# Turning the attention probabilities: TensorE transposes or one crossbar DMA a step

## The reference

```python
qk = jnp.einsum('bsd,btd->bst', q, k)                 # q = xn (8,512,256); 1024 keys
softmax_qk = jax.nn.softmax(qk * scale[:, None, :], axis=-1)   # scale: four rows of q, 1024 numbers a batch
attn = jnp.einsum('bst,btv->bsv', softmax_qk, v)
shared = new_gelu(xf @ Wfc_s + bfc_s) @ Wproj_s + bproj_s      # 256 -> 1024 -> 256
routed = sum over 8 experts e of gate_e * (new_gelu(xf @ Wfc[e] + bfc[e]) @ Wproj[e] + bproj[e])  # top 2 gates
out = x + attn + shared + routed
```

## Time and profile before

| | |
|---|---|
| median of three runs | 770.87 us |
| profiled execution, first to last instruction (span) | 769.0 us |
| the profiled execution's own time beside the span | the run's time is 770.87 us by the median: 1.9 us lie outside the span |
| TensorE busy / weight loads | 98% / 84% of the span |
| VectorE, ScalarE, GpSimd busy | 61%, 58%, 30% |
| DMA, mean over the span | 171 GB/s |

### The profile page before, as it was taken

The page is one execution under the profiler, slowest core; times in us unless marked ns, Lnnn a source line. Parts: engine busy times, 40 slices in busy tenths (PEclk is TensorE's granted clock), DMA queues, the critical chain, the costliest instruction groups (busy, mean ns, idle before and its releaser), DMA issues.

```text
span 769.0 us, 21389 instructions
## 1 busy us (share of the span) xinstructions
PE 756.3 (98%) x6963; PEld 645.5 (84%) x6963; DVE 470.6 (61%) x1161; ACT 449.6 (58%) x863; POOL 231.6 (30%) x272
## 2 busy tenths in 40 slices
PE   7999999999999999999999999999999999999998
PEld 6899866777777778999899988888888888888887
DVE  5887858888887797454544544444344444336776
ACT  6666546666668775556556565455544455544452
POOL 2445426656566752012122121121211221220000
PEclk9999999999999999999999999999999999999999
DMA  9657222657575958655523558546465646304565
GB/s 307 213 184 168 86 83 85 228 185 254 186 235 179 354 202 291 171 165 135 160 69 69 172 147 226 172 132 204 123 192 152 177 138 198 97 29 151 159 205 152
DMA packets 109949, 131.29 MB, mean 171 GB/s; under 512 B 64496, under 2 KB 91472, under 8 KB 103488
## 3 DMA queue, kind: packets, MB, share of 16 engines
q1 hardware_dynamic: 84784, 108.30, 46.4%
q0 software_dynamic: 6480, 17.77, 6.3%
q10 hardware_dynamic: 18624, 4.46, 2.9%
HBM read 89.32 MB, written 41.18 MB: 170 GB/s over the span
## 4 chain that ended last, share of the span: by engine, by line
PE 92%; DVE 3%; issue 2%; ACT 1%; DMA 1%; POOL 1%; ACTq 0%; DVEq 0%; POOLq 0%
PE ps_v L1413 32%; PE ps_h L1393 31%; PE ps_v L1573 11%; PE ps_h L1509 11%; PE ps_t L1523 4%; DMA slots_x<-x_split,pos_i 1%; PE ps_t L1344 1%; DVE h_split L1021 1%; PE ps_v L1471 0%; ACT h L804 0%; PE ps_v L1420 0%; PE ps_v L1344 0%; POOL slots_x L712 0%; PE ps_h L1445 0%; DVE v_split L1077 0%
## 5 line engine op out<-in xcount | busy, mean ns | idle before, releaser
L1021 DVE TENSOR_TENSOR h_split<-h,h_split 128x512 f16<-128x512 f32 (+1 forms) x224 | 142.3, 642 | 157.8 <-ACT h_split L810 157.6
L804 ACT ACTIVATE h<-ps_h,b_fc 128x256 f32<-128x256 f32 (+1 forms) x320 | 126.0, 444 | 156.2 <-PE ps_h L1393 156.2
L1393 PE MATMUL ps_h<-x_t,w_split 128*128 128x256 f16 (+1 forms) x1920 | 193.3, 261 | 0.1
L1413 PE MATMUL ps_v<-w_stage,h_split 128*128 128x256 f16 x1704 | 192.6, 273 | 0.2 <-DVE h_split L1021 0.2
L1393 PEld LDWEIGHTS ps_h<-x_t,w_split 128*128 128x128 f16 x1920 | 170.4, 98 | 17.4 <-issue 0.4
L1413 PEld LDWEIGHTS ps_v<-w_stage,h_split 128*128 128x128 f16 x1704 | 166.3, 98 | 19.5 <-issue 0.4
L748 POOL DMA_INDIRECT tokens_y<-prob,to_i x71 | 73.5, 1035 | 325.5 <-DMA tokens_y<-prob,to_i 177.6
L810 ACT CAST h_split<-h 128x512 f16<-128x512 f32 (+1 forms) x224 | 130.7, 584 | 10.0
L1509 PE MATMUL ps_h<-k_t,x_t 128*128 128x512 f16 x384 | 88.1, 379 | 1.7 <-issue 1.7
L1573 PE MATMUL ps_v<-v_split,p_t 128*128 128x256 f16 x768 | 88.9, 272 | 0.0
L804 ACT ACTIVATE h<-ps_h,b_t 128x256 f32<-128x256 f32 x128 | 53.5, 468 | 57.2 <-PE ps_h L1393 55.3
(11 more groups left out here) (162 smaller groups left out, 613.6 us busy)
## 6 DMA issues: line engine op xcount, KB each, us to landing
w_split<-wpack SPq DMA_DIRECT2D x17, 1024.0 KB, 5.7
w_stage<-wpack SPq DMA_DIRECT2D x17, 1024.0 KB, 5.3
wpack<-w_split SPq DMA_DIRECT2D x8, 1024.0 KB, 5.0
wpack<-h_split SPq DMA_DIRECT2D x8, 1024.0 KB, 5.0
y_rows<-tokens_y SPq DMA_DIRECT2D x32, 256.0 KB, 3.4
b_pj<-bias_e SPq DMA_DIRECT2D x40, 128.5 KB, 3.7
w_stage<-in_L_ffn_Wfc_dram SPq DMA_DIRECT2D x4, 1024.0 KB, 7.1
scale_b<-key_scale SPq DMA_DIRECT2D x8, 512.0 KB, 6.2
```

The lines of the kernel that those rows point to most:

```text
L804: ins = nc.scalar.activation(h32[:, hc, 0:n], ps_h[:, hc * TILE:hc * TILE + n], ACT.Gelu_apprx_tanh, bias=bias[:, hc:hc + 1], scale=1.0 / WS)
L1021: ve.tensor_tensor(h_split[par][:, 1, 2 * b:2 * b + 2, 0:n], h32[:, 2 * b:2 * b + 2, 0:n], h_split[par][:, 0, 2 * b:2 * b + 2, 0:n], ALU.s ...
L1393: ins = mm(ps_h[:, hc * TILE:hc * TILE + cols], wv[:, wl, c, hc * P:(hc + 1) * P], x[:, xl * DC + c, 0:cols], start=n == 0, stop=n == 3 * ...
L1413: ins = mm(ps_y[a][:, :], h_split[par][:, xl, c, a * P:(a + 1) * P], wv[:, wl, c, :], start=n == 0, stop=n == 3 * HC - 1)
```

## The change

The eight TensorE transposes of a step go away. ScalarE now casts `prob` straight into an SBUF tile `p_split` (hi), VectorE writes lo beside it (one instruction of 1024 columns in place of two of 512), and SyncE issues one DMA that turns both halves through the DMA crossbar, 128 rows of 4 KB, 512 KB, into `p_turned`, from which `values(u)` reads. `p_split` has two buffers, in the place of `w_shared[0]`; `p_turned` has three, the two old `p_t` and a part of `w_shared[1]`. The shared weights are therefore stored to DRAM (`w_rest`, 2 x 1024 KB) in the first stage and read back in the routed stage. The reciprocal of the row sum gets four buffers. The side work uses the PSUM tile `ps_t` again, which is free now, so its extra waits on `finish` go. The order within a step changes too: VectorE does `scale_scores(u+2)` first and `p_lo(u+2)` last in pass `u`, and ScalarE does `p_hi(u+2)` right after `exp(u+2)`, where before both halves of step `u` were made in pass `u`.

```diff
@@ dram
+    w_rest = dram("w_rest", (2 * P, 4096), f16)
@@ tiles
-        inv_sum = sb2("inv_sum", [P, 1], f32)
+        inv_sum = [sb(f"inv_sum{n}", [P, 1], f32) for n in range(4)]
+        p_split = [w_shared[0][:, n * 2 * KEYS:(n + 1) * 2 * KEYS] for n in range(2)]
+        p_turned = [t[:, :, :, :] for t in p_t] + [w_shared[1][:, 0:2 * KEYS].rearrange("p (h c n) -> p h c n", h=2, c=KC)]
-        side = [ps_v[:, a * 512:(a + 1) * 512] for a in range(2)]
...
+        lg_ps = misc[:, 0:SUB * 2 * EXPERTS]
+        rk_ps = misc[:, 32:32 + SUB * EXPERTS]
@@ sync
                 if i == 6:
                     load_job(2)
+                    for n in range(2):
+                        sp.dma_start(w_rest[n * P:(n + 1) * P, :], w_shared[n][:, :]).then_inc(s_rest_out, 16)
+            def turn_probs(u):
+                par, buf = u % 2, u % 3
+                if u == 2:
+                    wait_ge(sp, s_mm2, 2 * NA)
+                    wait_ge(sp, s_rest_out, 32)
+                if u >= 3:
+                    wait_ge(sp, s_pv, u - 2)
+                wait_ge(sp, s_phi, u + 1)
+                wait_ge(sp, s_plo, u + 1)
+                sp.dma_start_transpose(p_turned[buf].rearrange("p h c n -> p (h c) n"), p_split[par]
+                                       ).then_inc(s_p_in[buf], 16)
...
+            load_job(3)
+            turn_probs(0)
+            turn_probs(1)
             for u in range(QT):
...
                     load_slots(1, 1, True, first=True)
+                if u + 2 < QT:
+                    turn_probs(u + 2)
...
+            wait_ge(sp, s_pv, QT)
+            for n in range(2):
+                sp.dma_start(w_shared[n][:, :], w_rest[n * P:(n + 1) * P, :]).then_inc(s_rest_in, 16)
@@ scalar
             def p_hi(u):
                 par = u % 2
-                for kk in range(2):
-                    act.wait_ge(s_pt, 2 * u + kk + 1)
-                    if kk == 0 and u >= 2:
-                        act.wait_ge(s_pv, u - 1)
-                    nc.scalar.copy(p_t[par][:, 0, 4 * kk:4 * kk + 4, :],
-                                   ps_t[:, kk * 512:(kk + 1) * 512].rearrange("p (c n) -> p c n", n=P)).then_inc(s_phi, 1)
+                act.wait_ge(s_exp, u + 1)
+                if u >= 2:
+                    act.wait_ge(s_p_in[(u - 2) % 3], 16 * ((u - 2) // 3 + 1))
+                else:
+                    act.wait_ge(s_rest_out, 32)
+                nc.scalar.copy(p_split[par][:, 0:KEYS], prob[par][:, :]).then_inc(s_phi, 1)
...
             for u in range(QT):
-                p_hi(u)
...
                     exp(u + 2)
+                    p_hi(u + 2)
@@ vector
             def p_lo(u):
                 par = u % 2
                 dve.wait_ge(s_exp, u + 1)
-                if u >= 2:
-                    dve.wait_ge(s_fin, u - 1)
-                ve.reciprocal(inv_sum[par][:, :], row_sum[par][:, :]).then_inc(s_inv, 1)
-                for kk in range(2):
...
+                if u >= 4:
+                    dve.wait_ge(s_fin, u - 3)
+                ve.reciprocal(inv_sum[u % 4][:, :], row_sum[par][:, :]).then_inc(s_inv, 1)
+                dve.wait_ge(s_phi, u + 1)
+                ve.tensor_tensor(p_split[par][:, KEYS:], prob[par][:, :], p_split[par][:, 0:KEYS], ALU.subtract
+                                 ).then_inc(s_plo, 1)
...
             for u in range(QT):
+                if u + 2 < QT:
+                    scale_scores(u + 2)
                 if u >= 2:
                     finish(u - 2)
-                p_lo(u)
-                if u + 2 < QT:
-                    scale_scores(u + 2)
...
                 tables(u)
+                if u + 2 < QT:
+                    p_lo(u + 2)
@@ tensor
-            def transpose_probs(u):
-                pe.wait_ge(s_exp, u + 1)
...
-                    for c in range(4 * kk, 4 * kk + 4):
-                        ins = nc.tensor.transpose(ps_t[:, c * P:(c + 1) * P], prob[u % 2][:, c * P:(c + 1) * P], ident_f[:, :])
-                    ins.then_inc(s_pt, 1)
...
             def values(u):
...
+                for vl, pl in ((0, 0), (1, 0), (0, 1)):
+                    if n == 0:
+                        pe.wait_ge(s_p_in[buf], 16 * (u // 3 + 1))
+                    for c in range(KC):
+                        ins = mm(ps_y[par][:, :], p_turned[buf][:, pl, c, :], v_split[:, vl, c, :],
...
             for u in range(QT):
-                transpose_probs(u)
...
+            pe.wait_ge(s_rest_in, 32)
             for i in range(NA, SHARED):
```

More of the change, by code:

```diff
@@ L303, in moe_attention_block @@
         s_inv = sem("s_inv")
-        s_pt = sem("s_pt")
+        s_p_in = [sem(f"s_p_in{n}") for n in range(3)]
+        s_rest_out = sem("s_rest_out")
+        s_rest_in = sem("s_rest_in")
         s_phi = sem("s_phi")
@@ L1004, in slots_rest, with front_b @@
                 rb(ve.tensor_copy(pos_i[rpar][:, :], pos_r))
-            def front_b(norm=None, split=None, route=None, bank=misc):
+            def front_b(norm=None, split=None, route=None):
                 if norm is not None:
@@ L1335, in _, with transpose_quads @@
             TERMS = ((0, 0), (0, 1), (1, 0))
-            def transpose_quads(src, out=tr16, subs=range(SUB)):
+            def transpose_quads(src, subs=range(SUB)):
                 for hl in range(2):
@@ L1343, in transpose_quads @@
                             chunk = src[:, a, 0:ROW].rearrange("p (f k) -> p k f", k=2 * DC)
-                            ins = nc.tensor.transpose(out[:, n:n + P],
+                            ins = nc.tensor.transpose(tr16[:, n:n + P],
                                                       chunk[:, hl * DC + c, :], ident_h[:, :])
```

99 lines of the change are left out of this document (28 added, 71 removed).

## The result

The changed kernel takes 826.59 us (median of four runs, 826.18 to 827.43) against 771.00 us before: ratio 1.0726, 95% interval 1.071 to 1.0741, so 55.6 us slower. The prediction was 761.5 us, with a range to 797. The profiled execution spans 824.8 us.

The account below looks back on a forecast made before the run. TensorE bounds the kernel now; VectorE and the DMAs would then set passes of 5.85 us. Terms -8.6 + 2 - 2 - 0.8 = -9.4 us took the 769.0 span to 759.6, median 761.5 us; range 751 to 797.

Parts of the forecast that it names:

- With normalising and routing: VectorE's pass that normalises and routes: scaling, side work, finish with reciprocal and subtraction add up to 7.4 us.
- rival B: TensorE nearly reaches its own need: normalisation shrinks, transfers cost 1.5 us, passes take 5.5 us, time 753 us; chance 10%.
- Serial chain on VectorE 5.0, 5.1 and 7.4, mean 5.83: VectorE's us per attention pass, by kind: with tile split, with copy of a transposed tile, with normalising and routing.
- I take 1.8: DMA time of all engines for one 512 KB crossbar transfer: 1.8 us, near the two full-size rows.
- With 1.8 it is 5.8 us a pass, level with VectorE's 5.83. Both together I put at 5.85 us.: DMA engines in an attention pass: existing traffic 4.0 us at 348 GB/s plus one transfer, alongside VectorE.
- L of 4 to 7 us, threshold 9.4: Latency from the subtraction's end to the transfer's landing, expected hidden; up to 9.4 us costs nothing.
- +2 for the dense stretch: The 22nd to the last exponential: no saving in 10 passes, 2 us charged for five transfers in heavy DMA traffic.
- -2 for the tail: Last exponential to routed matmuls: two groups of transposes go, 1.8 us, landing before its product is due; saving 2 us.
- -0.8 for the start: Up to the third exponential: one group of transposes less, saving 0.8 us.
- D: Rival: DMA engines become the bound, deciding from 2.3 us a transfer; at 3 us, +18 us, 789 us; chance 20%.
- E: Rival: transfers land late, latency 12 us, queued behind 2 MB of weights; +25 us, 796 us; chance 8%.
- F: Rival: the transfer goes in 32 B pieces, 23.7 us a pass, +557 us, about 1330 us; chance 10%.

Follow-up runs that it names:

- e1: Changed kernel with GpSimd computing the next tile's square root before the scatter, not behind it: 804.14 us, ratio 1.0444.
- e2: Kernel before, no transfers, with its normalisation moved directly behind the finish: 786.15 us, ratio 1.0198.
- e12: Changed kernel without transfers or SyncE's waits for them, square root first, GpSimd's weight splits paced, shared weights stored earlier, rank product behind values product: 779.91 us.
- e4: Kernel before plus 32 crossbar transfers of 512 KB that nobody reads, and the store and reload of the shared weights: 819.17 us, ratio 1.064.
- e8: e4 with 32 plain SBUF copies of the same 512 KB in place of the crossbar transfers: 786.75 us, ratio 1.0203.
- e10: Changed kernel with square root first, shared weights stored one load earlier and rank product behind the values product: 799.99 us, ratio 1.0375.
- e15: e10 with a plain copy of the same 512 KB in place of each crossbar transfer, all waits kept: 786.52 us, ratio 1.0197.
- e14: Kernel before plus 32 crossbar transfers of 256 KB, half the size of e4's: 787.62 us, ratio 1.0227.

## Why the prediction was wrong, point by point

- *"With normalising and routing: 1.35 + (195.88 - 191.68 = 4.20) + 0.67 + 1.2 = 7.4."* This is the step that failed. It adds up VectorE's own instructions and puts the wait for the square root at nothing, without a reason; the pass took 12.3 us, 4.95 of them this wait. I judged the moved order on VectorE and TensorE alone. The normalisation moved forward, to right behind a finish, while GpSimd's split, scatter and square root stayed one serial chain of 10 us behind the finish before it. Its slack had been 0.4 us. The one place where I spoke of GpSimd's moment was the contention in rival B, and there only as a gain. No rival had "the normalisation waits for GpSimd". Shown by e1 (22.5 us) and e2 (15 us, no transfer). The extra waits on `finish` that go, which I also gave nothing, are not needed for it: e2 keeps them.
- *Serial chain on VectorE 5.0, 5.1 and 7.4, mean 5.83.* The durations were right (the low half 1.20 us, cast 1.05). Without transfers and with the order mended threes last 18.5 us, 6.18 a pass (e12), not 17.5. There VectorE still waits 1.3 us in each three for the root (7.7 us in 6), and in the split's pass one small cast takes 2.32 us instead of 0.17 beside GpSimd's split. Against that the normalisation, 2.18 us before, shrank to about 0.8, as rival B had it.
- *"I take 1.8" for a transfer.* Right for one that stands alone, 1.81 us (e4); that was luck in part, as no row showed one and the floor of 1.5 us was too high for a copy within SBUF (1.2 us, e8). In traffic a transfer fills more: its packets' times sum to 2.3 us alone and 3.0 in the mean of e4, with overlaps counted in.
- *"With 1.8 it is 5.8 us a pass, level with VectorE's 5.83. Both together I put at 5.85 us."* Failed. Full DMA engines do not serve a chain at no cost. In e4, at a pass of 6.39 us, the sum is (4.09 + 1.81) / 6.39 = 0.92 of the engines' time (0.64 x 6.39 = 4.09), and 0.96 was measured from 200 to 260 us: at that share the weight jobs fell behind from 250 us on. In e10, with a share of 1.09 (the view's shares can pass 1), a pass took about 6.7 us and 280 GB/s were moved, so mixed traffic did not reach the 348 GB/s that I used. In 5.85 us, 1.91 MB would have needed 326.
- *L of 4 to 7 us, threshold 9.4.* Landings in the changed kernel: 3.6 least, 4.6 median, 12.0 most. The median was right, the tail was not: behind a store and a load of 1 MB each SyncE's turning instruction itself lasted long:

```profile
312.49 9.20 SPq L510 DMA_TRANSPOSE w_shared<-w_shared  x1
```

- *+2 for the dense stretch.* +14.6 in the changed kernel, +6.4 with no transfer at all (e12). By e12's waits of VectorE for the exponential (7.0 us in two), the larger part of the latter is the serial way over ScalarE with two weight halves on it; that is read from the trace, and no run tests it. I had the 6.1 us of such a pass, but not that tables and finish stand behind it on VectorE.
- *-2 for the tail, -0.8 for the start.* +5.3 and +4.8. In the tail the slots load came late and TensorE waited 6.8 us, as in e12; I had not looked at what SyncE issues ahead of that load. At the start I had put the store of 2 MB at nothing, looking at the down-projection and not at the scatter whose landing a cast awaited (4.2 us).
- *The rivals.* D decided from 2.3 us a transfer. A lone one took 1.81 us, but by packets' times it is 2.3 to 3.0, and D's picture came true in e1, e4 and e10 (share 0.96 to 1.10, late weights or late landings). It comes second in the changed kernel, behind the wait for the root, and is decided by the sum of all traffic in a pass and by the crossbar's form, which e8 and e15 show at 32 and 13.5 us. E's waits for a late transfer make 15 us in the changed kernel. F was far off. The granted clock under 1.00, which I named as a sign, did add: 4.12 to 4.64 us for 2.78 in a third of the passes.
- *Not tried:* whether more of the crossbar's cost lies in its packets (about 2100 each: queue 1 has 67136 more than before) or in SyncE's long issue. What in the end stage of e12 would have to move to win back its loss was not tried either.

## What to carry to other kernels

When a change moves an instruction forward in a hand-ordered pass, look up for each of its inputs the time it was ready and the time it was used, on every engine, also the ones that the change does not touch: a wait that is not in the profile can be 0.4 us away from being in it. A set of engines whose predicted share comes to over 0.9 is a bound, with late transfers, and not a level tie: at 0.90 the pace held here up to the 28th finish (e14), at 0.96 it broke behind the 21st (e4). And price a transfer by its form, a copy and a transposing transfer of the same bytes apart.
